# A cross attention stage on one Trainium2 core: the small product of each key tile is issued ahead of the product with the values

## What is computed

```
xn, ln_lat = layer_norm(x, g1, b1), layer_norm(latents, g2, b2)
q = ln_lat @ Wq
k, v = split(concatenate([xn, ln_lat], axis=1) @ Wkv)      # heads = 16, dim_head = 64
weight = einsum('bhld,bhnd->bhln', q * scale, k * scale)
weight = where(full_mask, weight, -finfo.max)
weight = softmax(weight)
out = einsum('bhln,bhnd->bhld', weight, v)
return out.reshape(b, l, heads * dim_head) @ Wout
```

## Time and profile before

| what | value |
|---|---|
| median of 3 runs (lowest, highest) | 3316.15 us (3311.12, 3316.19) |
| the profiled execution, its time | 3314.16 us |
| its span in the profile | 3312.4 us |
| TensorE matmuls busy | 2950.3 us, 89% of the span, 18490 instructions |
| VectorE busy | 1918.0 us, 58% |
| ScalarE busy | 1456.2 us, 44% |
| GpSimd busy | 1202.9 us, 36% |
| the changed loop | about 214 us to 1256 us, a third of the span |

### The profile page before, as it was taken

One profiled execution on the slowest core, in us unless ns is written; L12 is line 12 of the kernel. 1 busy time (PEld: TensorE's weight loads), 2 busy tenths in 40 slices (PEclk: granted clock), 3 DMA queues, 4 the chain that ended last, 5 costly groups with the idle time before them and its releaser, 6 DMA issues. The chain is left out here.

```text
span 3312.4 us, 48893 instructions
## 1 busy us (share of the span) xinstructions
PE 2950.3 (89%) x18490; PEld 1974.5 (60%) x18490; DVE 1918.0 (58%) x3101; ACT 1456.2 (44%) x2394; POOL 1202.9 (36%) x1001
## 2 busy tenths in 40 slices
PE   7879999999999997999998787799687888899978
PEld 6645555555555545888885566799565565344345
DVE  6656566665665655224225875556457758666566
ACT  3334444444444444333323264677432635355554
POOL 0135666666666670000003531466133412122232
PEclk9979999999999998999999898899899999799989
DMA  1100000000000001111111003676400000000010
GB/s 58 54 1 1 1 1 1 1 1 1 1 1 1 1 1 53 51 48 41 46 32 32 21 1 128 200 201 194 112 1 1 19 10 1 2 1 1 1 33 26
DMA packets 117130, 114.51 MB, mean 35 GB/s; under 512 B 22827, under 2 KB 102725, under 8 KB 116901
## 3 DMA queue, kind: packets, MB, share of 16 engines
q1 hardware_dynamic: 103173, 97.66, 9.5%
q0 software_dynamic: 7488, 9.48, 1.6%
q10 hardware_dynamic: 6240, 4.26, 0.4%
HBM read 100.81 MB, written 11.47 MB: 34 GB/s over the span
## 5 line engine op out<-in xcount | busy, mean ns | idle before, releaser
L827 POOL TENSOR_TENSOR acc<-acc,pf 128x512 f32<-128x512 f32 (+1 forms) x448 | 563.9, 1281 | 254.6 <-ACT pf L954 254.6
L1011 DVE TENSOR_REDUCE mxa<-ps 128x1 f32<-128x512 f32 x512 | 327.2, 681 | 229.2 <-PE ps L873 227.3
L954 ACT ACTIVATE pf<-ps 128x512 f32<-128x512 f32 x512 | 277.9, 595 | 318.9 <-PE ps L848 293.5
L861 PE MATMUL ps<-pf,v 128*64 128x512 f32 (+1 forms) x1152 | 311.4, 619 | 0.0
L3741 ACT ACTIVATE pT<-ps 128x1024 f32<-128x1024 f32 (+1 forms) x192 | 154.1, 811 | 136.0 <-PE ps L3658 135.4
L3754 DVE TENSOR_REDUCE mx<-ps 128x2 f32<-128x1024 f32 (+1 forms) x192 | 175.2, 952 | 46.7 <-PE ps L3645 38.0
L1208 POOL TENSOR_TENSOR x<-x,ys 128x256 f32<-128x256 f32 x16 | 11.8, 739 | 508.6 <-DVE ys L1413 508.6
L873 PE MATMUL ps<-kH,qH 64*128 64x512 f32 x512 | 158.1, 441 | 23.7 <-DVE mc L1019 18.6
L1862 POOL TENSOR_TENSOR e<-e,sm 128x1232 f32<-128x1232 f32 x48 | 107.9, 2248 | 171.1 <-DVE sm L2132 171.1
L2592 DVE TENSOR_TENSOR w_lo<-w2a,w_hi 128x2048 fp32r<-128x2048 f32 x39 | 89.4, 2292 | 101.4 <-ACT w_hi L2479 101.4
L2391 PE MATMUL ps<-xT,w1r 128*128 128x128 f32 x1248 | 148.1, 278 | 0.0
(11 more groups left out here) (550 smaller groups left out, 7404.5 us busy)
## 6 DMA issues: line engine op xcount, KB each, us to landing
w1r<-in_f_w SPq DMA_DIRECT2D x39, 1024.0 KB, 5.2
w_raw<-in_c_h SPq DMA_DIRECT2D x32, 512.0 KB, 4.2
w2a<-in_f_w SPq DMA_DIRECT2D x8, 1024.0 KB, 13.0
w_raw<-in_c_w SPq DMA_DIRECT2D x32, 128.0 KB, 2.3
x<-in_x SPq DMA_DIRECT2D x1, 2048.0 KB, 8.2
moe_rows<-rowbuf ACTq DMA_DIRECT2D x4, 512.0 KB, 8.2
moe_acc<-x ACTq DMA_DIRECT2D x1, 2048.0 KB, 9.5
x<-moe_acc SPq DMA_DIRECT2D x4, 512.0 KB, 5.5
```

Source lines behind the costliest of these rows:

```text
L827: pool.tensor_tensor(now[0:r, :], now[0:r, :], pf[0:r, n % RING, a, :], ALU.add).then_inc(added.sem, 1)
L861: ins = pe.matmul(g.bk(3)[SIDE[a], :], v[0:r, u // 2 % 2, t, u % 2 * P + a * HD:u % 2 * P + (a + 1) * HD], pf[0:r, n % RING, a, :], start= ...
L954: act.activation(pf[0:r, n % RING, a, :], g.bk(bk.bank[f"s{n}_{a}"])[0:r, :], ACT.Exp, bias=bias)\
L1011: dve.tensor_reduce(mxa[:, q % 2, half, a, j:j + 1], g.bk(4 + a), AXX, ALU.max).then_inc(bk.release(f"m{q}_{i}_{a}"), 1)
```

## The change

In the loop of TensorE in the second block of `stage_l0_xattn` the line `values(n)` moves behind the loop over the small products of the step. Nothing is added or removed, and the lists of the other engines stay as they are.

```
@@ -932,9 +932,9 @@
                         scores(n + 1)
                     for m in maxima_in(q, t, 0):
                         maxima(*m)
-                    values(n)
                     for o in others_in(q, t):
                         other(*o)
+                    values(n)
                     for m in maxima_in(q, t, 1):
                         maxima(*m)
                 for o in tail:
```

## The result

| what | before | changed |
|---|---|---|
| median of 5 runs | 3311.61 us | 3327.7 us |
| lowest, highest | 3310.56, 3316.19 | 3325.17, 3330.47 |
| the profiled execution | 3314.16 us | 3330.47 us |
| first turn to last output product (start to start, profile) | 213.07 to 1254.27: 1041.2 us | 212.46 to 1267.04: 1054.6 us |

The ratio is 1.0043, with a 95% interval of 1.0029 to 1.0058: 14 us slower on 3311.6 (the medians lie 16.1 us apart). The last row is what I call the loop in the following: from the start of the first turn (L898) to the start of the last output product (L894). It holds nothing of the other stages and is therefore the sharper measure: in the two profiles, one execution each, it grew by 13.4 us. Prediction: 13.8.

A forecast was written before the change was run, and what follows sets the result against it. TensorE's own list was taken to set the pace; stalls of 7.0 + 2.2 + 1.4 + 2.2 + 1.0 = 13.8 us on the 3316.15 us median gave 3330.0 us. Own range 3323 to 3338, 8 in 10 3319 to 3341.

The forecast's parts named there:

- The bound: TensorE's list in the loop sets the pace, busy 960.5 of 980 us; stalls put into it add up.
- The switch between products: Each step's sum stays 2.91 us in the new order: 0 us, bounds 23.5 us less or more over 235 places.
- A: Rival: the switch into the values is cheap, 0.10 us back at each of 235 places, 3306.4 us; chance 7%.
- C: Rival: the unseen switch into the values costs 0.10 us more at 235 places, 3353.4 us; chance 8%.
- C's falling clock: Within the dearer rival: the granted clock falls in the new idle times, also slower; given little chance.
- Small products that wait for no one: q, k, v, sums and second half of y can start earlier without waiting, tightest 1.2 us left: 0 us.
- The first half of y: Step 5, waits for oT: 7.0 us in even chunks, 2.2 in chunks 3, 7, ... 27, 1.4 in 29 and 30.
- The turn: Step 6, waits for nm: 0.32 us in chunks 1, 5, ... 25, 2.2 us; 1.0 us in chunk 0.
- Sum: All stalls in TensorE's list together: 7.0 + 2.2 + 1.4 + 2.2 + 1.0 = 13.8 us slower.
- The absolute forecast: Whole kernel: 3330.0 us, the 13.8 us put on the 3316.15 us median of the runs shown.

The follow-up runs named there:

- both_back: Changed kernel with the first half of y and the turn put back behind the values; ratio 0.9997 to the kernel before, loop 1041.7 us.
- turn_back: Changed kernel with only the turn (step 6) put back behind the values; ratio 1.0030 to the kernel before, loop 1052.0 us.
- y_back: Changed kernel with only the first half of y (step 5) put back behind the values; ratio 1.0029 to the kernel before, loop 1049.8 us.
- rec_early: Changed kernel with nm made by one reduction and all four reciprocals in VectorE's step 2; ratio 1.0008 to the kernel before, loop 1043.2 us.
- rec_fit: rec_early, but chunks 29 and 30 keep their reciprocals in steps 2 and 3; ratio 0.9985 to the kernel before, loop 1037.8 us.
- direct_nm: Changed kernel with nm made by one reduction, its sign in ScalarE's copy; ratio 1.0027 to the kernel before, loop 1050.4 us.
- scale_first: Changed kernel with VectorE's scaling (oT) ahead of the key projection's low part in step 4; ratio 1.0046 to the kernel before, loop 1054.3 us.

## Why the prediction was right

**The bound** (TensorE's list, so that every stall counts in full): right. The losses per chunk add up to the loop's, and nothing is given back.

**The switch between products, 0 us with bounds of 23.5 either way:** right. 2.91 us in both orders, and both_back shows no loss with 172 moves. Rivals A and C are gone with it; so is C's falling clock, since the changed kernel has 1.00 in its steady part.

**Small products that wait for no one, 0 us:** right, by the same kernel. One reading was off: the tightest of them, with 1.2 us left, is not a key projection behind another (2.9 us left), but the first key or value projection of a chunk behind the query projection.

**The first half of y, 10.6 us:** 0.47 to 0.53 us in the even chunks for 0.50, 0.27 to 0.32 for 0.31, and 0.58 and 0.64 for 0.68. turn_back measures the term by itself: 10.8.

**The turn, 2.2 us and 1.0 in chunk 0:** 0.27 to 0.34 for 0.32, 0.93 for 1.0. That y's stall hides the turn's in the even and every second odd chunk was the step that made the sum smaller than the count of its parts; y_back (8.6, when 3.2 would be the independent sum) shows that it was needed.

**Sum:** 13.8 against 13.4 in the loop and 14 by the ratio. By term the losses per chunk add up to 7.0 (y, even chunks), 2.0 (y, chunks 3, 7, ...), 1.2 (y, chunks 29 and 30), 2.2 (turn) and 0.9 (chunk 0), for 7.0, 2.2, 1.4, 2.2 and 1.0 forecast: no term was saved by another, but for 0.1 us of chunk 14 at the turn, which stands in the first. The absolute forecast, 3330.0, lies 2.3 us over the median measured: of the five runs of before the later ones put its median at 3311.6 instead of 3316.15, 4.5 us lower. The change was sized on the trace, the base on three runs. That the absolute number fits so well is partly luck: the base was 4.5 us too high, the step between the medians (16.1) 2.3 us larger than forecast.

**What the steps left out:** y has a second releaser, its PSUM bank, freed by the low part of the key projection 0.6 us ahead of `oT`. For the forecast it made no difference, but the sentence that y waits "for `oT`" was half of the cause, and the first attempt to mend it failed on the other half.

## What to carry to other kernels

A product that waits for nothing, standing right ahead of one that waits, is worth as much as it covers; before moving it, list for every product behind it how long ago its releasers ended, all of them, and price the move as the difference of those times plus the 0.15 us of the hand-over. Stalls of one list are not independent: the first one moves the later ones out of reach of their own releasers, so remove or add them in order of time. And the same table read the other way shows where a cover is missing: two moves of that kind, with the single reduction for `nm`, took 1.5% off this kernel.

## What the runs showed of the hardware

**The clock after a stall.** In rec_early the stall of 1.94 us in chunk 29 (to 1179.35) was followed, from 1181.2 to 1188.0 us, by the lower granted clock, 0.50 (1.2 GHz). Busy time by stretch, before, during and after (columns as above, the clock is the third number from the end):

```profile
1170.00:1177.00 7.00, 7.00 (x44) 2.96 (x40) 4.81 (x8) 3.48 (x7) 4.92 (x4) 1.00 0.00 0
1182.00:1188.00 6.00, 6.00 (x18) 2.87 (x18) 3.19 (x6) 1.40 (x3) 4.16 (x4) 0.50 0.00 0
1188.00:1195.00 7.00, 7.00 (x37) 2.87 (x36) 0.69 (x1) 2.84 (x5) 4.78 (x4) 1.00 0.01 2
```

Between 1182 and 1188 us the starts of successive pairs of score matmuls are 0.4 to 0.6 us apart instead of 0.23 to 0.34:

```profile
1183.82 0.79 PE L851 MATMUL ps<-qH,kH 64*128 64x512 f32 x2
1184.42 0.63 PE L851 MATMUL ps<-qH,kL 64*128 64x512 f32 x2
```

By the steps, about 2.7 of chunk 29's 4.2 us were lost in steps 4 and 5, behind the stall and at the lower clock. The same stall in chunk 30 (to 1211.76) was followed by 0.50 from 1211.9 to 1215.3 us, and step 4 lost 1.2 us there. The same stretch of rec_fit, which lacks the stall, stays at 1.00:

```profile
1160.00:1195.00 35.00, 32.86 (x185) 16.81 (x184) 20.52 (x33) 13.91 (x25) 21.77 (x18) 1.00 0.00 1
```

But the length of a stall alone doesn't decide it. In the changed kernel TensorE idled 2.32 us in chunk 0, and the clock stayed:

```profile
240.00:243.00 3.00, 0.68 (x7) 0.24 (x3) 2.77 (x3) 1.08 (x2) 3.00 (x4) 1.00 0.00 0
243.00:250.00 7.00, 6.43 (x41) 2.98 (x41) 1.54 (x3) 3.54 (x6) 3.53 (x3) 1.00 0.00 0
```

What differs between the two places was not tried, so it stays open. Stalls of 0.6 us and below never moved the clock in any of these kernels; the 4.9 us in front of the last output product did in all of them.

**GpSimd holds up small VectorE operations:** they take up to 1.28 us instead of 0.17 (kernel before, L1025), and whether they do depends on the operands: pairs of SBUF inputs, and a multiplication from SBUF to SBUF the one time that it ran beside an addition, but in 31 such cases of direct_nm no reduction.

**The hand-over** from the end of a VectorE operation to the start of the matmul that waited for it is 0.15 us in all 31 stalls on `oT` and `nm` of the changed kernel's loop. For a bank there are two values: 0.15 us too in the 30 waits of the maxima for the bank that VectorE's `mc` (L1019) lets go, but 0.06 us in the 14 waits of y for its bank in scale_first (the 572.32 above). What makes the difference wasn't tried.
